# Attention stage of a vision tower: where the short slots of the score pass stand among the steps of the key pass

## The chip, the cores and the metric

The program runs on one core of one Trainium2 chip. The metric is device time in microseconds of that core. The kernel before ran three times: 1735.34, 1737.99 and 1738.87 us, median 1737.99 us. One further execution was recorded by the hardware profiler.

## The reference, cut to what matters

The reference is a small vision tower on 4 sequences of 513 tokens with 192 channels. It has a token embedding, a recurrent mixer with a feed-forward part, an attention layer with a routed expert feed-forward part, a spiking attention, and a last attention layer with a feed-forward part. The two softmax attention layers have 12 heads of 16 channels; the change lies in the function that computes them. For one layer:

```python
scores = jnp.einsum('bqhd,bkhd->bhqk', q, k) / jnp.sqrt(jnp.float32(Dh))
attn = jax.nn.softmax(scores, axis=-1)
ao = jnp.einsum('bhqk,bkhd->bqhd', attn, v).reshape(B, S, D)
```

The second layer (`a = softmax(q k^T * scale)`, `o = a v`) has the same form, sizes and code.

## The kernel before, in words

`attention` (L1922) runs twice, once as `att0` and once as `att1`. The 12 heads of a batch entry are taken four at a time, so one attention is 12 groups of (batch entry, four heads). Every group goes through two passes.

The first pass finds the maximum of the scores of each query. TensorE multiplies queries by keys (`scores`, L2024, 128 queries by 512 keys, one PSUM bank each), and VectorE reduces each bank to one maximum per query (L2149). A group has 16 such units, taken two at a time in 8 full *slots*. Two short slots go with them. `last_queries` (L2037, the unit `ends`) scores the 513th query of the four heads in one bank, which takes VectorE one reduction (L2154). `last_keys` (L2047, the unit `last`) scores all queries against the 513th key, after which VectorE merges all maxima into the tile `mexp` with small instructions (L2162, L2167, L2169). A group has 10 slots (`SLOTS`), numbered u = 0 to 9. Then `turn` (L2065) transposes the maxima of the group on TensorE, and `copy_max` (L1979) copies them as an extra row into the queries: VectorE copies for one half of the partitions, ScalarE for the other. So the second pass gets scores from which the maximum is already subtracted. The banks of units `s`, `ends`, `last` and `max` are the three banks 0 to 2, used in turn in the order of the list `ring`; `free` (L2008) makes TensorE wait until the bank's former content has been read.

The second pass multiplies keys by queries (`keys`, L2085, half of the queries at a time), takes the exponential on ScalarE (L2198, L2195), and multiplies by the values on TensorE (`values`, L2110), adding up in bank 3. It has 10 *steps* per group, 0 to 9: steps 0 to 3 and 5 to 8 have two units each (two calls of `keys`, two exponentials of 514 columns), steps 4 and 9 are short and have one unit (one call for the 513th key, one exponential of 257 columns, L2195). The 18 units of a group are numbered i = 0 to 17; unit 8 and unit 17 are the short ones. `keys` of a unit waits until the exponential of the unit two before it is done, since there are two pairs of banks for it. `values` of a step comes two steps later (`BEHIND`). ScalarE also copies the sums of each half out of bank 3 (`copy_sums`, L2177) after units 3 and 12, and the first `values` of a half waits for that copy (L2118).

TensorE's order is written out by a loop over steps (L2131 to L2140): step t issues `keys`, then the two score units of slot LEAD + t, then `keys` of the second unit, then `values` of step t - 2, then `others` (L2075): `last_queries`, `last_keys` or `turn`, if slot LEAD + t is one of u = SLOTS - 2, SLOTS - 1 or 1. The first LEAD slots are issued ahead of the loop. LEAD is 13 before, so step k of a group has slot u = k + 3 (modulo 10) beside it: `last_queries` (u = 8) stands in step 5, `last_keys` (u = 9) in step 6, `turn` (u = 1) in step 8, and the short steps 4 and 9 carry the full slots u = 7 and u = 2. On ScalarE, `copy_max` for the next group stands after the exponential of unit 15, which is the first unit of step 8. VectorE takes everything in the order of `ring` (L2144).

While `att0` runs, GpSimd splits expert weights into halves beside it (L2487, L2489, L2491, one after the other); `att1` runs without that.

Of the kernel before, what the change touches and what calls it, by code (L numbers as in the profile page):

```python
# [44 lines left out]
SLOTS = (2 * NT + EXPERTS * 127) // 128  # L45
# [1876 lines left out]
def attention(c, name, q2, kT, v, aT, att, wts, experts=False):  # L1922
# [2 lines left out]

    nc = c.nc
    NK = AT
    HALF = T // 2 + 1  # L1930
# [5 lines left out]
    G = len(groups)  # L1936
    with ExitStack() as ctx:
# [9 lines left out]
        NS = len(S_UNITS)  # L1947
        SLOTS = NS // 2 + 2
# [3 lines left out]
        STEP_OF = [i for i, step in enumerate(STEPS) for _ in step]  # L1952
        NB, NT_ = len(UNITS), len(STEPS)
        assert NT_ == SLOTS
        LEAD = SLOTS + 3
        BEHIND = 2
        mc = (mc_v, mc_s)
        acc = c.bank[3]

        ring = []  # L1960
        for n in range(G * SLOTS + 2):
            g, u = divmod(n, SLOTS)
            if g < G and u < SLOTS - 2:
                ring += [("s", g * NS + 2 * u), ("s", g * NS + 2 * u + 1)]
            ring += [("ends", g)] if u == SLOTS - 2 else []
            ring += [("last", g)] if u == SLOTS - 1 else []
            ring += [("max", g - 1, 0), ("max", g - 1, 1)] if u == 1 and g else []
        place = {unit: at for at, unit in enumerate(ring)}

        def bank_of(unit):  # L1970

            return c.bank[place[unit] % 3]
# [6 lines left out]
        def copy_max(eng, copy, g, gi, e):  # L1979

            b, j = groups[g]
            eng.wait_ge(mt, 2 * g + gi + 1)
            bank = bank_of(("max", g, gi))
            r = 64 * e + 32
            copy(q2[r:r + 1, 2 * j + gi, b * T:b * T + KEYS], bank.bitcast(F16)[r:r + 1, 0:KEYS]).then_inc(mc[e], 1)
            copy(q2[r:r + 1, 2 * j + gi, b * T + KEYS:(b + 1) * T], bank[r:r + 1, KEYS - 1:KEYS]).then_inc(mc[e], 1)

        halves = ExpertHalves(c, ctx) if experts else None
        with nc.Block() as block:
            @block.sync  # L1990
            def _(sp):
                if experts:
                    halves.load(sp)
# [13 lines left out]
            def _(pe):  # L2007
                def free(unit):  # L2008

                    at = place[unit]  # L2010
                    if at < 3:
                        return
                    before = ring[at - 3]
                    if before[0] == "s":
                        pe.wait_ge(maxed, before[1] + 1)
                    elif before[0] == "ends":
                        pe.wait_ge(ends_max, before[1] + 1)
                    elif before[0] == "last":
                        pe.wait_ge(placed, 3 * before[1] + 3)
                    else:  # L2020
                        for e in range(2):
                            pe.wait_ge(mc[e], 2 * (2 * before[1] + before[2] + 1))

                def scores(s):  # L2024
                    g, u = divmod(s, SLOTS)
                    if g >= G or u >= SLOTS - 2:
                        return
                    b, j = groups[g]
                    for n in (g * NS + 2 * u, g * NS + 2 * u + 1):
                        gi, k, e = S_UNITS[n % NS]  # L2030
                        q0 = b * T + 128 * k
                        r = slice(64 * e, 64 * e + 64)
                        free(("s", n))
                        pe.matmul(bank_of(("s", n))[:, 0:KEYS], q2[r, 2 * j + gi, q0:q0 + 128],  # L2034
                                  kT[r, 2 * j + gi, b * T:b * T + KEYS], start=True, stop=True).then_inc(scored, 1)

                def last_queries(g):  # L2037
                    b, j = groups[g]
                    free(("ends", g))
                    for gi in range(2):  # L2040
                        for e in range(2):
                            r, to = slice(64 * e, 64 * e + 64), 32 * (2 * gi + e)
                            ins = pe.matmul(bank_of(("ends", g))[to:to + 32, 0:KEYS], q2[r, 2 * j + gi, ends_of(g)],
                                            kT[r, 2 * j + gi, b * T:b * T + KEYS], start=True, stop=True)
                    ins.then_inc(ends, 1)

                def last_keys(g):  # L2047
                    b, j = groups[g]
                    if g == 0:
                        pe.wait_ge(init, 2)  # L2050
                    free(("last", g))
                    bank = bank_of(("last", g))
                    for gi in range(2):
                        for k in range(NK):
                            q0, at = b * T + 128 * k, 2 * (gi * NK + k)
                            pe.matmul(bank[:, at:at + 2], q2[:, 2 * j + gi, q0:q0 + 128], last[:, 2 * j + gi, b, :],
                                      start=True, stop=True)
                    for gi in range(2):
                        for e in range(2):
                            r, to = slice(64 * e, 64 * e + 64), 32 * (2 * gi + e)  # L2060
                            ins = pe.matmul(bank[to:to + 32, 4 * NK:4 * NK + 1], q2[r, 2 * j + gi, ends_of(g)],
                                            last[r, 2 * j + gi, b, e:e + 1], start=True, stop=True)
                    ins.then_inc(lasts, 1)

                def turn(g):  # L2065
                    pe.wait_ge(placed, 3 * g + 3)
                    for gi in range(2):
                        free(("max", g, gi))
                        bank = bank_of(("max", g, gi))
                        for k in range(NK):  # L2070
                            pe.transpose(bank.bitcast(F16)[:, 128 * k:128 * k + 128], mexp[:, g % 2, gi, k, :], idh[:, :])
                        pe.matmul(bank[:, KEYS - 1:KEYS], mexp[:, g % 2, gi, NK, :], one[:, 0:1], start=True, stop=True
                                  ).then_inc(mt, 1)

                def others(s):  # L2075

                    g, u = divmod(s, SLOTS)
                    if u == SLOTS - 2 and g < G:
                        last_queries(g)
                    if u == SLOTS - 1 and g < G:  # L2080
                        last_keys(g)
                    if u == 1 and 1 <= g <= G:
                        turn(g - 1)
# [43 lines left out]

                for s in range(LEAD):
                    scores(s)
                    others(s)  # L2130
                for t in range(G * NT_ + BEHIND):  # L2131
                    g, step = divmod(t, NT_)
                    if g < G:
                        keys(g, FIRST[step])
                        scores(LEAD + t)
                        if len(STEPS[step]) == 2:
                            keys(g, FIRST[step] + 1)
                    if t >= BEHIND:
                        values(t - BEHIND)
                    others(LEAD + t)  # L2140

# [33 lines left out]
            @block.scalar  # L2175
            def _(act):
                def copy_sums(n):  # L2177
                    b, j = groups[n // 2]
                    act.wait_ge(summed, (NK + 1) * (n + 1))
                    if n % 2:  # L2180
                        act.wait_ge(copied, n)
                    at = b * T + START[n % 2]
                    act.copy(aT[:, j, at:at + HALF], acc[:, 0:HALF]).then_inc(copied, 1)  # L2183

                for gi in range(2):
                    copy_max(act, act.copy, 0, gi, 1)
                for n in range(G * NB):
                    g, i = divmod(n, NB)
                    half, k, gi = UNITS[i]
                    act.wait_ge(keyed, n + 1)  # L2190
                    if n >= RING:
                        g0, i0 = divmod(n - RING, NB)
                        act.wait_ge(summed, g0 * NT_ + STEP_OF[i0] + 1)
                    if k == NK:
                        act.activation(p[:, n % RING, 0, :], c.pair[2 + n % 2][:, 0:HALF], ACT.Exp, scale=scale  # L2195
                                       ).then_inc(expd, 1)
                    else:
                        act.activation(p[:, n % RING, :, :],  # L2198
                                       c.pair[2 + n % 2][:, :].rearrange("p (e q) -> p e q", e=2)[:, :, 0:HALF],
                                       ACT.Exp, scale=scale).then_inc(expd, 1)  # L2200
                    if i == NB - 3 and g + 1 < G:
                        for gi in range(2):
                            copy_max(act, act.copy, g + 1, gi, 1)
                    if i == 3 and g:
                        copy_sums(2 * g - 1)
                    if i == 12:
                        copy_sums(2 * g)
                copy_sums(2 * G - 1)
# [1133 lines left out]
```

## Time and profile before

| | |
|---|---|
| time of the runs | 1735.34, 1737.99, 1738.87 us |
| profiled execution: own time | 1737.85 us |
| profiled execution: span | 1736.1 us |
| TensorE matmul busy | 1454.7 us (84%) |
| VectorE busy | 1240.4 us (71%) |
| ScalarE busy | 1015.9 us (59%) |
| GpSimd busy | 407.1 us (23%) |
| VectorE reductions of scores, L2149 | 234.9 us in 384 |
| ScalarE exponentials, L2198 | 211.9 us in 384 |
| TensorE values, L2124 | 123.5 us in 1536 |
| TensorE keys, L2106 | 112.3 us in 768 |
| TensorE scores, L2034 | 107.8 us in 384 |

The span is the time from the first to the last instruction of the profiled execution; its own time is as the other runs are timed. Attention `att0` takes the stretch from 761.5 us to about 940 us of the span, and `att1` the one from about 1404 us to about 1577 us. Busy sums of the two attentions are not told apart in the rows of the table that name a line: each is over both.

### The profile page before, as it was taken

The numbers are of one execution on the slowest core, as the hardware profiler recorded it, in microseconds if no ns is written. First come the engines' busy times: TensorE is split into PE (matmuls) and PEld (weight loads), VectorE is DVE, ScalarE is ACT, GpSimd is POOL, SyncE is SP. The second block draws the span as 40 slices with busy tenths as digits, with TensorE's granted clock in tenths as the row PEclk, the third lists the DMA queues.
The fourth block names the chain that finished last, engine by engine and source line by source line (L and its number), as shares of the span: only waits on it lengthen the run. The fifth ranks groups of instructions, "written<-read, shape, count | busy, mean of one in ns | idle before, by whom it ended". The sixth has DMA issues, their size and how long they took to land. (4 is left out here: it accounts for less than half of the span.)

```text
span 1736.1 us, 36685 instructions
## 1 busy us (share of the span) xinstructions
PE 1454.7 (84%) x14444; PEld 1083.2 (62%) x14444; DVE 1240.4 (71%) x2561; ACT 1015.9 (59%) x1867; POOL 407.1 (23%) x414
## 2 busy tenths in 40 slices
PE   5889898698489789899999719995697999999795
PEld 5889898598455757643335618884586643336474
DVE  5988898389789557468885657874656378885466
ACT  6988898343668264547886306663102448884565
POOL 0000000101556220349920117763000310000200
PEclk9999999689699989879999759998697879999897
DMA  5110100100000100015500732121200000000101
GB/s 147 29 42 29 38 2 11 45 1 1 1 9 2 32 4 15 1 59 183 171 30 2 213 118 60 58 63 34 70 1 14 1 1 2 2 2 2 35 1 37
DMA packets 52750, 67.98 MB, mean 39 GB/s; under 512 B 11536, under 2 KB 41490, under 8 KB 52579
## 3 DMA queue, kind: packets, MB, share of 16 engines
q1 hardware_dynamic: 46022, 50.30, 9.6%
q0 software_dynamic: 3840, 9.18, 1.8%
q10 hardware_dynamic: 2716, 6.14, 1.4%
q8 instruction: 116, 1.90, 0.5%
q14 instruction: 56, 0.45, 0.1%
HBM read 46.97 MB, written 18.65 MB: 38 GB/s over the span
## 5 line engine op out<-in xcount | busy, mean ns | idle before, releaser
L340 PE MATMUL banks<-tok_wT,feature_halves 128*128 128x192 f16 x2592 | 229.3, 249 | 23.7 <-DVE feature_halves L366 12.5
L2149 DVE TENSOR_REDUCE att_max<-banks 128x1 f32<-128x512 f32 x384 | 234.9, 682 | 6.9 <-PE banks L2034 5.9
L340 PEld LDWEIGHTS banks<-tok_wT,feature_halves 128*128 128x128 f16 x2592 | 216.8, 99 | 33.0 <-DVE feature_halves L366 18.3
L2198 ACT ACTIVATE att_p<-banks 128x514 f32<-128x514 f32 x384 | 211.9, 600 | 30.9 <-PE banks L2106 22.8
L366 DVE TENSOR_TENSOR feature_halves<-features,feature_halves 128x2048 f16<-128x2048 f32 x54 | 123.4, 2286 | 6.9 <-ACT feature_halves L463 6.9
L2124 PE MATMUL banks<-att_p,att_v 128*32 128x257 f32 x1536 | 123.5, 394 | 0.5 <-ACT att_aT L2183 0.3
L2106 PE MATMUL banks<-att_q,att_kT 64*128 64x257 f16 x768 | 112.3, 282 | 6.0 <-ACT att_p L2198 3.1
L2034 PE MATMUL banks<-att_kT,att_q 64*128 64x512 f16 x384 | 107.8, 416 | 9.8 <-PEq L1793 4.0
L135 PE MATMUL banks<-ones 128*128 128x256 f16 x654 | 88.7, 294 | 28.4 <-PEq L252 13.7
L463 ACT CAST feature_halves<-features 128x2048 f16<-128x2048 f32 x54 | 102.3, 1894 | 11.3 <-PE banks L340 10.5
L135 PEld LDWEIGHTS banks<-ones 128*128 128x128 f16 x654 | 65.7, 105 | 46.4 <-issue 25.3
L2106 PEld LDWEIGHTS banks<-att_q,att_kT 64*128 64x128 f16 x768 | 36.7, 94 | 85.8 <-ACT att_p L2198 51.8
L2923 ACT COPY slot_xT<-banks 128x512 f16<-128x512 f16 x40 | 23.4, 586 | 94.4 <-PE banks L2873 91.7
L2886 PE MATMUL banks<-slot_xT,expert_w 128*128 128x128 f16 x1200 | 75.3, 222 | 3.0 <-ACT slot_xT L2923 2.9
L741 POOL MEMSET xT<- 1x4104 f32 x1 | 3.5, 3519 | 313.2 <-POOLq L252 313.2
L2886 PEld LDWEIGHTS banks<-slot_xT,expert_w 128*128 128x128 f16 x1200 | 70.6, 99 | 6.1 <-ACT slot_xT L2923 5.9
L355 DVE SCALAR_TENSOR_TENSOR angle_rest<-raw_T,freq,turns 128x1024 f32<-128x1024 f32 x54 | 69.1, 1279 | 6.2 <-ACT turns L240 5.7
L2902 PE MATMUL banks<-expert_w,slot_hidden_halves 128*128 128x192 f16 x720 | 65.9, 246 | 8.9 <-DVE slot_hidden_halves L2971 8.4
L2902 PEld LDWEIGHTS banks<-expert_w,slot_hidden_halves 128*128 128x128 f16 x720 | 58.2, 97 | 12.9 <-issue 9.8
L2840 POOL DMA_INDIRECT slot_x<-token_rows,slot_comes x40 | 46.8, 1169 | 74.5 <-POOLq L2541 62.7
L2034 PEld LDWEIGHTS banks<-att_kT,att_q 64*128 64x128 f16 x384 | 31.1, 95 | 48.8 <-DVE att_max L2149 20.5
L456 ACT ACTIVATE features<-angle_abs,half_pi 128x1024 f32<-128x1024 f32 x54 | 61.5, 1138 | 0.0
(493 smaller groups left out, 3487.2 us busy)
## 6 DMA issues: line engine op xcount, KB each, us to landing
expert_w_in<-in_L_ffn_w_dram SPq DMA_DIRECT2D x16, 576.0 KB, 4.6
expert_w_halves<-expert_w_halves SPq DMA_DIRECT2D x32, 288.0 KB, 2.4
tok_w<-in_L_tok_W_dram ACTq DMA_DIRECT2D x4, 1152.0 KB, 7.2
expert_w2s<-expert_w_halves SPq DMA_DIRECT2D x1, 4608.0 KB
expert_y<-expert_out SPq DMA_DIRECT2D x6, 513.0 KB
expert_w1s<-expert_w_halves SPq DMA_DIRECT2D x2, 1536.0 KB
raw<-in_x_dram SPq DMA_DIRECT2D x2, 1152.0 KB, 5.5
expert_w1s<-expert_w_halves SPq DMA_DIRECT2D x3, 768.0 KB
```

The costliest lines, as they stand in the source:

```text
L135: pe.matmul(c.bank[bank][:, 0:256], ones[:, 0:128], ones, start=True, stop=True)
L340: ins = pe.matmul(c.bank[t // 2][:, (t % 2) * D:(t % 2 + 1) * D], fh[:, s, q, z, t * 128:(t + 1) * 128], wT[:, y, k, 6 * q + wf, :], start ...
L355: own.did(dve.scalar_tensor_tensor(fr[:, n % 2, :], rT[:, k, hf * HALF:(hf + 1) * HALF], freq_col(k, f), fm[:, n % 2, :], ALU.mult, ALU.su ...
L366: dve.tensor_tensor(fh[:, s, :, 1, :], feat[:, s, :, :], fh[:, s, :, 0, :], ALU.subtract).then_inc(flow, 1)
L463: act.copy(fh[:, s, :, 0, :], feat[:, s, :, :]).then_inc(fhigh, 1)
L2034: pe.matmul(bank_of(("s", n))[:, 0:KEYS], q2[r, 2 * j + gi, q0:q0 + 128], kT[r, 2 * j + gi, b * T:b * T + KEYS], start=True, stop=True).th ...
L2106: ins = pe.matmul(c.pair[2 + n % 2][:, 512 * e:512 * e + HALF], kT[r, 2 * j + gi, k0:k0 + 128], q2[r, 2 * j + gi, queries], start=True, st ...
L2124: ins = pe.matmul(acc[32 * hh:32 * hh + 32, 0:HALF], v[:, b, k, 4 * j + hh, :], p[:, (n + hh // 2) % RING, hh % 2, :], start=(k == 0), sto ...
L2149: dve.reduce_max(mx[:, n // NS % 2, 2 * gi + e, k:k + 1], bank_of(unit)[:, 0:KEYS], X).then_inc(maxed, 1)
L2198: act.activation(p[:, n % RING, :, :], c.pair[2 + n % 2][:, :].rearrange("p (e q) -> p e q", e=2)[:, :, 0:HALF], ACT.Exp, scale=scale).the ...
L2886: ins = pe.matmul(ps, ws[:, s, at:at + 128], xt[:, s, b, :], start=(k == 0), stop=(k == len(TERMS) - 1))
L2902: ins = pe.matmul(ps, hh[:, s, a, f, :], w2[:, f, b, :], start=(f == k == 0), stop=(f == NF - 1 and k == 2))
```

## The change

The unit `ends` moves from u = 8 to u = 4 (`ENDS = NK`), and the score units of u = 5 to 8 follow it (`first_score`). LEAD grows from 13 to 15. With that, step k has slot u = k + 5 (modulo 10) beside it: `last_keys` (u = 9) stands in step 4, `turn` (u = 1) in step 6, `last_queries` (u = 4) in step 9, and the eight full slots stand in the eight full steps. ScalarE's `copy_max` moves from after unit 15 to after unit 11, the first unit of step 6. No instruction is added or taken away.

```diff
-        LEAD = SLOTS + 3
+        ENDS = NK
+        LEAD = SLOTS + NK + 1
         BEHIND = 2
...
+        def first_score(g, u):
+
+            return g * NS + 2 * (u - (u > ENDS))
+
         ring = []
         for n in range(G * SLOTS + 2):
             g, u = divmod(n, SLOTS)
-            if g < G and u < SLOTS - 2:
-                ring += [("s", g * NS + 2 * u), ("s", g * NS + 2 * u + 1)]
-            ring += [("ends", g)] if u == SLOTS - 2 else []
+            if g < G and u not in (ENDS, SLOTS - 1):
+                n0 = first_score(g, u)
+                ring += [("s", n0), ("s", n0 + 1)]
+            ring += [("ends", g)] if u == ENDS and g < G else []
             ring += [("last", g)] if u == SLOTS - 1 else []
             ring += [("max", g - 1, 0), ("max", g - 1, 1)] if u == 1 and g else []
...
                 def scores(s):
                     g, u = divmod(s, SLOTS)
-                    if g >= G or u >= SLOTS - 2:
+                    if g >= G or u in (ENDS, SLOTS - 1):
                         return
                     b, j = groups[g]
-                    for n in (g * NS + 2 * u, g * NS + 2 * u + 1):
+                    for n in (first_score(g, u), first_score(g, u) + 1):
...
                 def others(s):
 
                     g, u = divmod(s, SLOTS)
-                    if u == SLOTS - 2 and g < G:
+                    if u == ENDS and g < G:
                         last_queries(g)
...
-                    if i == NB - 3 and g + 1 < G:
+                    if i == NB - 7 and g + 1 < G:
                         for gi in range(2):
                             copy_max(act, act.copy, g + 1, gi, 1)
```

## Rows read from the trace of the kernel before

**Rows 1.** The page, part 1: busy us, share of the span, instructions.
```profile
PE 1454.7 (84%) x14444; PEld 1083.2 (62%) x14444; DVE 1240.4 (71%) x2561; ACT 1015.9 (59%) x1867; POOL 407.1 (23%) x414
```
**Rows 2.** Timeline of VectorE in att1: start us, us, instruction, [idle before <-releaser].
```profile
1506.48 0.69 DVE L2154 TENSOR_REDUCE att_max_last<-banks 128x1 f32<-128x512 f32 x1 [0.53 <-PE banks L2043]
1508.08 0.16 DVE L2162 TENSOR_TENSOR att_max_last<-att_max_last,banks 128x1 f32<-128x1 f32 x1 [0.91 <-PE banks L2061]
...
1508.30 0.23 DVE L2169 TENSOR_SCALAR att_max_placed<-consts,att_max_last 128x4 f16<-128x4 f32 x1
...
1511.87 7.30 DVE L2149 TENSOR_REDUCE att_max<-banks 128x1 f32<-128x512 f32 x12
1519.69 0.69 DVE L2154 TENSOR_REDUCE att_max_last<-banks 128x1 f32<-128x512 f32 x1 [0.53 <-PE banks L2043]
```
**Rows 3.** Timeline of TensorE in the same group of att1.
```profile
1507.40 0.35 PE L2056 MATMUL banks<-att_last_keys,att_q 128*128 128x2 f16 x8
...
1507.80 0.28 PE L2106 MATMUL banks<-att_q,att_kT 64*128 64x257 f16 x2
...
1508.91 0.28 PE L2106 MATMUL banks<-att_q,att_kT 64*128 64x257 f16 x2
...
1510.17 0.40 PE L2071 MATMUL banks<-att_ident,att_max_placed 128*128 128x128 f16 x4
...
1510.75 0.29 PE L2099 MATMUL banks<-att_q,att_kT 64*32 64x257 f16 x4
...
1511.81 0.64 PE L2124 MATMUL banks<-att_p,att_v 128*32 128x257 f32 x8
1512.56 0.29 PE L2106 MATMUL banks<-att_q,att_kT 64*128 64x257 f16 x2
...
1517.23 0.29 PE L2099 MATMUL banks<-att_q,att_kT 64*32 64x257 f16 x4
```
**Rows 4.** Timeline of ScalarE in the same group.
```profile
1510.62 0.58 ACT L1985 COPY att_q<-banks 1x512 f16<-1x512 f16 x1 [0.78 <-PE banks L2072]
...
1511.82 0.60 ACT L2198 ACTIVATE att_p<-banks 128x514 f32<-128x514 f32 x1
1512.31 0.38 ACT L2195 ACTIVATE att_p<-banks 128x257 f32<-128x257 f32 x1
...
1514.99 0.38 ACT L2183 COPY att_aT<-banks 128x257 f32<-128x257 f32 x1
```
**Rows 5.** Timeline of TensorE, last group of att0: a short step without scores, then one more.
```profile
932.44 0.29 PE L2099 MATMUL banks<-att_q,att_kT 64*32 64x257 f16 x4
932.66 0.64 PE L2124 MATMUL banks<-att_p,att_v 128*32 128x257 f32 x8
933.24 0.40 PE L2106 MATMUL banks<-att_q,att_kT 64*128 64x257 f16 x4
```
**Rows 6.** Timeline of VectorE in att0, beside GpSimd's work: two groups.
```profile
787.34 2.62 DVE L2169 TENSOR_SCALAR att_max_placed<-consts,att_max_last 128x4 f16<-128x4 f32 x1
...
829.78 0.78 DVE L2169 TENSOR_SCALAR att_max_placed<-consts,att_max_last 128x4 f16<-128x4 f32 x1
```
**Rows 7.** Timeline of GpSimd in att0, at the same places.
```profile
786.80 3.12 POOL L2487 TENSOR_SCALAR expert_w_in<-expert_w_in 128x1152 f32<-128x1152 f32 x1
789.99 1.14 POOL L2489 CAST expert_w_halves<-expert_w_in 128x1152 f16<-128x1152 f32 x1
791.22 2.37 POOL L2491 TENSOR_TENSOR expert_w_halves<-expert_w_in,expert_w_halves 128x1152 f16<-128x1152 f32 x1
...
827.41 3.12 POOL L2487 TENSOR_SCALAR expert_w_in<-expert_w_in 128x1152 f32<-128x1152 f32 x1
```
**Rows 8.** Timeline of TensorE, att1: the first keys after the leading slots.
```profile
1418.01 0.72 PE L2106 MATMUL banks<-att_q,att_kT 64*128 64x257 f16 x2
```
**Rows 9.** Timeline of ScalarE, att1: the first exponentials.
```profile
1418.10 1.28 ACT L2198 ACT_TABLE_LOAD   x1
1419.40 2.82 ACT L2198 ACTIVATE att_p<-banks 128x514 f32<-128x514 f32 x5
```
## The prediction

> **What bounds the kernel now.** I read the page first: TensorE is busy 84% of the span, VectorE 71%, ScalarE 59% [rows 1]. The change touches only the two attentions, so what counts is what ends last inside one group of them. I went to the timelines of the three engines over one group of att1, which GpSimd leaves alone. The reader is to see a pattern that repeats: the reduction of `ends` starts at 1506.48 and the next at 1519.69, so a group takes 13.21 us [rows 2]. There are 24 such groups, 22 with a turn of maxima inside the steps (11 in each attention).
>
> VectorE is idle 0.53 + 0.91 = 1.44 us of a group, before the reduction of `ends` and before the merge after `last` [rows 2]. Those are the steps in which it gets no full slot. It reduces a bank each 7.30/12 = 0.61 us, so a full slot is 1.22 us to it. TensorE takes 1.11 us for a full step with scores (1507.80 to 1508.91) [rows 3] and hardly pauses, except in one place. That place is the turn: it starts at 1510.17, ScalarE, idle for 0.78, starts its copies at 1510.62 and is back at exponentials only at 1511.82 [rows 3, 4]. TensorE's keys of the next group start at 1512.56, 0.14 after the end of that exponential (1511.82 + 0.60 = 1512.42): they wait for it. Meanwhile TensorE had `values` of step 7 to do, issued at 1511.81 [rows 3]. So a group is no engine's pure work; it is a round of three engines with one stop at the copies of maxima and smaller ones at the short slots.
>
> **The change part by part.** No instruction comes or goes, so the sum is one of waits. I lay the group out anew with the distances of the rows, starting from `last_keys`, set at 1507.40 in both.
>
> From `last_keys` to the turn nothing changes. Before, steps 7 and 8 follow it; after, steps 5 and 6, which have the same contents (two units, one full slot). `last_keys` takes 0.40 (to 1507.80), the next step 1.11, and the turn again starts at 1510.17 and ends at 1510.75 [rows 3]. ScalarE copies after the first unit of that step in both versions, so it is again free at 1511.82 [rows 4]. VectorE's merge and its reductions keep their order, too.
>
> Then comes what is new. Before, the step after the turn is the short step 9: keys of unit 17, a full slot, `values`. The keys that need the exponential delayed by the copies stand behind those `values`. After, it is the full step 7: keys of unit 13, a slot, *keys of unit 14*, `values` of step 5. Keys of unit 14 need the exponential of unit 12, which is the one behind the copies, so they start at 1512.56, where step 0 starts today. `values` of step 5, 0.58 of work [rows 5], are queued behind them. They also need `copy_sums` of the first half, which stands right behind unit 12's exponential: start 1512.31 (the next instruction starts 0.49 after the exponential), 0.38 long, 0.14 for the signal, so 1512.83 [rows 4]; after keys at 1512.56 + 0.22 [rows 5] it would be 1512.78. Step 7 ends at 1512.83 + 0.58 = 1513.41, where before step 9 was over at 1512.56. Slip: 0.85.
>
> From there to the next `last_keys`, before: 1507.40 + 13.21 - 1512.56 = 8.05. After: step 8 at 1.11; step 9 without scores at 0.22 + 0.58 [rows 5] and `last_queries` at no more than the 0.40 of `last_keys`, 1.20; steps 0 to 3 at 1517.23 - 1512.56 = 4.67 [rows 3]; step 4 up to `last_keys` at 0.22 + 0.58 = 0.80. Sum 7.78, so 0.27 is gained by the waits that went from the former steps 5 and 6. That is all that the alignment gives: a short step costs TensorE its `values` in any case, and VectorE's 1.44 idle time was not what TensorE waited for.
>
> One more term. Today the slot of step 0 is begun by VectorE at 1511.87 + 1.22 = 1513.09, 0.53 after the step [rows 2, 3]. After, the reduction of `ends` stands before it and can't begin before `last_queries` is done, at the start of step 0; it takes 0.61, and VectorE's 1.22 per slot is more than TensorE's 4.67/4 = 1.17 per step. TensorE is three banks ahead at most. I bound this by 0 (lag absorbed) and 0.25 (0.2 later at step 0, then 0.05 a step), and take 0.10, nearer to nothing, since the waits of ScalarE lie in the same steps. Per group: 0.85 - 0.27 + 0.10 = 0.68; ends 0.50 - 0.15 (should step 8 and 0 win back another 0.4 of the slip, for ScalarE has two exponentials in hand) = 0.15 below, and 0.85 above. Times 22: 15.0 us (3.3 to 18.7).
>
> LEAD 15 puts one full slot and one `ends` more ahead of the first keys: three reductions, 1.83. Behind them stand the first keys, now at 1418.01 [rows 8]. But the first exponential starts at 1419.40, behind the table load from 1418.10 [rows 9], which no keys are needed for; some 0.9 of the 1.83 lies beside it. I take 1.0 for each attention, 2.0 in all (0 to 4; the two slots less at the end had nobody waiting).
>
> In att0 there is GpSimd. L2169 alone takes 0.23 [rows 2]. Beside GpSimd it took 2.62 and ended at 789.96, and 0.78 and ended at 830.56 [rows 6]; GpSimd's L2487 ended at 789.92 and 830.53 [rows 7]. So it waits out the GpSimd instruction under way. The two places are 40.60 apart, three groups at 13.53, and GpSimd's own are 40.61 apart, six rounds at 6.77: a group of 13.21 plus a wait has locked to two rounds, at a wait of 0.55, of which 13.53 - 13.21 = 0.32 shows. A group of 13.9 is over 13.54 and can't lock so. Then L2169 falls anywhere in three instructions with hardly a gap [rows 7]: mean wait (3.12² + 1.14² + 2.37²)/(2 x 6.77) = 1.23, of which 1.0 shows. Seven groups run beside GpSimd. Before: 2.39 - 0.23 = 2.2 for the first and 6 x 0.32, 4.1; after: 7.0. Plus 3 us (-3, if it falls in gaps, to +10, if it meets the start of the instructions each time).
> The Trainium skill, page "SBUF — State Buffer", section "Who interferes with whom", says that VectorE and GpSimd share a pair of ports as an exclusive lock, that `tensor_scalar` in a two-port mode takes it, and that `tensor_reduce` never does. By that rule, the trace agrees: L2169 is a TENSOR_SCALAR, the reductions kept 0.61. By the rule the phase between the two engines decides, and the sum would be that of the rows; by the 0.23 of the undisturbed row it would be 3 us lower.
>
> Sum: 15.0 + 2.0 + 3 = 20 us on the profiled execution's own 1737.85, which is the median of 1737.99 but for 0.14. Forecast 1758.
>
> **The rivals.**
> *The slip is won back.* 0.5 of the waits in the 8.05 us after it go (8.05 against 7.5 of pure steps): 0.35 a group, 22 x 0.35 = 7.7, leads 2: 1747. For it: ScalarE has units 13 and 14 in hand. Against: TensorE's own steps take 1.11 whatever ScalarE has.
> *GpSimd's lock.* L2169 meets the start of each instruction: about 1.9 more shown wait in five of seven groups, +9.5 for my +3: 1765. For it: 13.85 is close over 13.54, so it would drift by 0.3 a group into the next instruction. Against: it can only happen while GpSimd works.
> *Faster, the other side.* VectorE sets the group. If the small waits of TensorE for banks are really VectorE's 1.44, filling the short steps takes off up to that, and the stop at the copies is covered as now: 0.85 slip less 1.44 is -0.6 a group, x 22 = -13: 1725. It decides if TensorE's full steps today are stretched by VectorE by over 0.1 each. For it: VectorE's 1.22 per slot is over TensorE's 1.11. Against: steps 0 to 3 together are only 0.23 over 4 x 1.11.
> *No effect.* The slip of 0.58 for `values` is just work shifted, and all of it comes back: 1738. Against: it leaves TensorE idle from about 1511.8 to 1512.83, where now it works.
>
> **How the numbers follow.** Forecast 0.48, won back 0.20, lock 0.13, faster 0.12, no effect 0.07. Slower by over 0.2% (3.5 us, about what a measurement tells from none) is 0.81, within it 0.07, faster 0.12. The range leaves out the faster case and no effect, 0.19: from 1741 (3.3 for the groups, nothing else) to 1770 (18.7 + 4 + 9.5). The likeliest case alone: 1750 to 1764.
>
> **What would show it.** In att1, a group of 13.8 to 13.9 instead of 13.21. In step 7 (the step after the turn), a pause of TensorE of about 0.7 ahead of the second keys, waiting for L2198, and `values` behind it at 2.1 from the turn's end. ScalarE's copies, the exponential and `copy_sums` in one row. VectorE idle some 0.5 before each short slot still, plus some 0.8 in step 8. L2169 of changing length in att0. The prediction is wrong if the group is below 13.3: then step 7's `values` didn't wait, or the steps today are stretched by VectorE. It is wrong in size if `values` start at once after the keys but steps 0 to 3 shrink below 4.5.

## The result

The changed kernel takes 1764.55 us (median of 4 runs, 1761.2 to 1766.32), the kernel before 1736.66 us (4 runs, 1735.01 to 1738.87). The ratio is 1.0159, 95% interval 1.0136 to 1.0181: slower, by 28 us between the medians. The forecast was 1758 with a range of 1741 to 1770. The profiled execution of the changed kernel has a span of 1763.4 us, 27.3 us over that of before. Its page, part 1 (answers to [rows 1]):

```profile
span 1763.4 us, 36685 instructions
PE 1470.3 (83%) x14444; PEld 1080.6 (61%) x14444; DVE 1250.6 (71%) x2561; ACT 1020.2 (58%) x1867; POOL 410.4 (23%) x414
```

The shares of the span show nothing of where the time went: the engines have the same instructions and wait more. So I measured each attention in the profiled executions, from the end of VectorE's last copy into `kT` to the end of ScalarE's last copy of sums:

| | before | after | difference |
|---|---|---|---|
| ahead of att0 | 759.9 | 761.2 | +1.3 |
| att0 | 180.1 | 200.7 | +20.6 |
| between the attentions | 461.9 | 457.5 | -4.4 |
| att1 | 175.6 | 184.8 | +9.2 |

The stretch between the attentions isn't touched by the change; over the profiled executions of this study it lay anywhere from 453.7 to 462.8 us. Differences of whole runs of a few us carry that noise, so what follows goes by groups and attentions.

**A group in att1.** VectorE's timeline of the changed kernel (answers to [rows 2]). The reduction of `ends` (now L2161) starts 13.89 us apart, where it was 13.21; VectorE now idles three times, 0.54, 0.75 and 0.78.

```profile
1509.27 0.69 DVE L2161 TENSOR_REDUCE att_max_last<-banks 128x1 f32<-128x512 f32 x1 [0.54 <-PE banks L2050]
...
1515.49 0.16 DVE L2169 TENSOR_TENSOR att_max_last<-att_max_last,banks 128x1 f32<-128x1 f32 x1 [0.75 <-PE banks L2068]
...
1521.34 1.29 DVE L2156 TENSOR_REDUCE att_max<-banks 128x1 f32<-128x512 f32 x2 [0.78 <-PE banks L2041]
1523.16 0.69 DVE L2161 TENSOR_REDUCE att_max_last<-banks 128x1 f32<-128x512 f32 x1 [0.54 <-PE banks L2050]
```

TensorE's timeline from one `last_keys` to the next (answers to [rows 3]). The turn ends at 1518.16, where step 7 begins; its score units are held up (0.91), its second keys start at 1519.88 behind a pause of 0.60, and `values` at 1520.23.

```profile
1514.80 0.35 PE L2063 MATMUL banks<-att_last_keys,att_q 128*128 128x2 f16 x8
...
1518.16 0.29 PE L2113 MATMUL banks<-att_q,att_kT 64*128 64x257 f16 x2
1518.38 0.91 PE L2041 MATMUL banks<-att_kT,att_q 64*128 64x512 f16 x2
1519.88 0.29 PE L2113 MATMUL banks<-att_q,att_kT 64*128 64x257 f16 x2 [0.60 <-ACT att_p L2205]
1520.23 0.64 PE L2131 MATMUL banks<-att_p,att_v 128*32 128x257 f32 x8
1520.80 0.29 PE L2113 MATMUL banks<-att_q,att_kT 64*128 64x257 f16 x2
...
1523.04 0.28 PE L2113 MATMUL banks<-att_q,att_kT 64*128 64x257 f16 x2
...
1527.90 0.29 PE L2106 MATMUL banks<-att_q,att_kT 64*32 64x257 f16 x4
...
1528.69 0.35 PE L2063 MATMUL banks<-att_last_keys,att_q 128*128 128x2 f16 x8
```

ScalarE's timeline of the same place (answers to [rows 4]): four copies of maxima, then the exponential of unit 12, then the copy of the sums.

```profile
1518.02 0.58 ACT L1992 COPY att_q<-banks 1x512 f16<-1x512 f16 x1 [0.78 <-PE banks L2079]
...
1519.22 0.60 ACT L2205 ACTIVATE att_p<-banks 128x514 f32<-128x514 f32 x1
1519.72 0.37 ACT L2190 COPY att_aT<-banks 128x257 f32<-128x257 f32 x1
```

**A group in att0.** The starts of the reduction of `ends` beside GpSimd's work are 15.13, 18.25, 15.51, 18.48, 15.37 and 16.40 us apart, and 13.9 after it; before, they were 15.30 apart once and then 13.5 to 13.7. The 15.13 is the first group after the leading slots, which is about as long in att1 (15.58); the other five are the ones lengthened. VectorE's TENSOR_SCALAR (L2176, answers to [rows 6]) waits for GpSimd's instruction (answers to [rows 7]), and TensorE for it:

```profile
802.04 2.89 DVE L2176 TENSOR_SCALAR att_max_placed<-consts,att_max_last 128x4 f16<-128x4 f32 x1
```
```profile
801.78 3.12 POOL L2494 TENSOR_SCALAR expert_w_in<-expert_w_in 128x1152 f32<-128x1152 f32 x1
```
```profile
804.99 0.73 PE L2041 MATMUL banks<-att_kT,att_q 64*128 64x512 f16 x2 [2.06 <-DVE att_max_placed L2176]
```

And there is more in these groups than the wait. The next rows give the busy time by stretches of the changed kernel: start and end, length, busy us and instructions of TensorE, its weight loads, VectorE, ScalarE and GpSimd, then the granted clock of TensorE, DMA share, GB/s. The first row is the stretch around the pause, the second the one behind it. TensorE is busy 2.74 of 4.80 us at a granted clock of 1.00, and then the clock is 0.51, near its lower level of 1.2 GHz, for 6.7 us. The same happened at 840.5 to 847, behind the wait of L2176 at 835.80, and not at 874 to 880, behind the one at 869.65.

```profile
801.50:806.30 4.80, 2.74 (x32) 0.84 (x32) 4.48 (x7) 1.69 (x3) 4.65 (x4) 1.00 0.73 246
806.90:813.60 6.70, 6.32 (x48) 1.58 (x45) 3.64 (x9) 4.50 (x11) 6.55 (x4) 0.51 0.51 176
...
840.50:847.00 6.50, 6.12 (x48) 1.63 (x45) 3.89 (x9) 4.62 (x11) 6.35 (x4) 0.53 0.59 181
...
874.00:880.00 6.00, 5.20 (x64) 2.03 (x60) 4.62 (x11) 4.69 (x12) 5.85 (x4) 1.00 0.27 101
```

### The profile page after: what moved, and what is told of

Read it like the earlier page. It is cut to its first block and busy times, and to the rows that moved or that the text cites. A ratio compares the mean times of both kernels' runs of the same rounds, so it can differ in the third digit from the quotient of the medians.

```text
span 1763.4 us, 36685 instructions
## 1 busy us (share of the span) xinstructions
PE 1470.3 (83%) x14444; PEld 1080.6 (61%) x14444; DVE 1250.6 (71%) x2561; ACT 1020.2 (58%) x1867; POOL 410.4 (23%) x414
## 5 line engine op out<-in xcount | busy, mean ns | idle before, releaser
L2156 DVE TENSOR_REDUCE att_max<-banks 128x1 f32<-128x512 f32 x384 | 237.7, 682 | 24.1 <-PE banks L2041 23.4
L340 PE MATMUL banks<-tok_wT,feature_halves 128*128 128x192 f16 x2592 | 228.2, 248 | 23.3 <-DVE feature_halves L366 12.2
L2113 PE MATMUL banks<-att_q,att_kT 64*128 64x257 f16 x768 | 120.2, 287 | 15.9 <-ACT att_p L2205 15.6
L2131 PE MATMUL banks<-att_p,att_v 128*32 128x257 f32 x1536 | 127.8, 406 | 2.0 <-ACT att_aT L2190 0.7
L2041 PE MATMUL banks<-att_kT,att_q 64*128 64x512 f16 x384 | 114.9, 424 | 16.5 <-DVE att_max_placed L2176 8.6
L2909 PE MATMUL banks<-expert_w,slot_hidden_halves 128*128 128x192 f16 x720 | 66.3, 246 | 10.5 <-DVE slot_hidden_halves L2978 8.9
L2847 POOL DMA_INDIRECT slot_x<-token_rows,slot_comes x40 | 53.2, 1329 | 73.2 <-POOLq L2548 61.5
L1827 PE MATMUL banks<-att_qkv_w,xT 96*128 96x384 f32 (+3 forms) x136 | 57.4, 548 | 5.6 <-POOL att_qkv_parts L1802 3.1
```

Source lines behind the costliest of these rows:

```text
L340: ins = pe.matmul(c.bank[t // 2][:, (t % 2) * D:(t % 2 + 1) * D], fh[:, s, q, z, t * 128:(t + 1) * 128], wT[:, y, k, 6 * q + wf, :], start ...
L2113: ins = pe.matmul(c.pair[2 + n % 2][:, 512 * e:512 * e + HALF], kT[r, 2 * j + gi, k0:k0 + 128], q2[r, 2 * j + gi, queries], start=True, st ...
L2131: ins = pe.matmul(acc[32 * hh:32 * hh + 32, 0:HALF], v[:, b, k, 4 * j + hh, :], p[:, (n + hh // 2) % RING, hh % 2, :], start=(k == 0), sto ...
L2156: dve.reduce_max(mx[:, n // NS % 2, 2 * gi + e, k:k + 1], bank_of(unit)[:, 0:KEYS], X).then_inc(maxed, 1)
L2909: ins = pe.matmul(ps, hh[:, s, a, f, :], w2[:, f, b, :], start=(f == k == 0), stop=(f == NF - 1 and k == 2))
```

## The experiments

Each is timed against runs of the kernel before made beside it (medians 1735.71 for e1 to e4, 1738.85 for e5 to e8, 1740.08 for e9; e9 has two runs of its own, the others four to ten). The ratio is the one on record, which differs from the quotient of the two medians by up to 0.002. The group is the distance of the starts of the `ends` reduction in the steady part of att1; att0 and att1 are from one profiled execution each.

| kernel | time, us | ratio to before, 95% | group | att0 | att1 |
|---|---|---|---|---|---|
| before | 1736.66 | | 13.21 | 180.1 | 175.6 |
| after | 1764.55 | 1.0159 (1.0136 to 1.0181) | 13.89 | 200.7 | 184.8 |
| e1, sums copied first | 1761.0 | 1.0162 (1.0127 to 1.0196) | 13.84 | 194.3 | 186.9 |
| e2, maxima copied after unit 12 | 1737.6 | 1.0018 (0.9997 to 1.0038) | 13.21 | 179.6 | 177.2 |
| e3, after with fused merge | 1749.37 | 1.0084 (1.0060 to 1.0108) | 13.82 | 183.9 | 183.9 |
| e4, before with fused merge | 1725.25 | 0.9944 (0.9925 to 0.9962) | 13.15 | 174.6 | 174.4 |
| e5, turn back in step 8 | 1741.08 | 1.0010 (0.9998 to 1.0023) | 13.1 | 183.9 | 177.3 |
| e6, e5 and maxima after unit 16 | 1726.62 | 0.9939 (0.9920 to 0.9958) | 12.52 | 179.4 | 170.4 |
| e7, before, maxima after unit 16 | 1736.53 | 0.9982 (0.9956 to 1.0008) | 13.18 | 179.7 | 174.4 |
| e8, e6 with fused merge | 1722.19 | 0.9907 (0.9890 to 0.9924) | 12.45 | 170.0 | 169.5 |
| e9, after with filler matmuls | 1786.52 | 1.0271 (1.0211 to 1.0330) | 15.27 | 208.3 | 202.4 |

**e1: is it the copy of the sums that `values` wait for?**

```diff
+                    if i == 11:
+                        copy_sums(2 * g)
                     if i == NB - 7 and g + 1 < G:
...
-                    if i == 12:
-                        copy_sums(2 * g)
```

> The changed kernel, with the copy of the first half's sums moved on ScalarE from behind the exponential of unit 12 to ahead of the copies of maxima (after unit 11). Theory A (the keys of unit 14 wait for the exponential of unit 12, which is queued behind the copies of maxima, and the values stand behind these keys): the sums are now free early, but the keys of unit 14 start no earlier, and the values follow them 0.35 us later as today; the group of att1 stays at 13.8 to 13.9 us and the time at 1762 to 1765 us. Rival B (what stops TensorE in step 7 is the wait of the values for the copied sums): the pause behind the turn goes, the group falls by 0.5 to 0.8 us to 13.1 to 13.4, the time by 11 to 18 us to about 1750.

The group is 13.84, so B falls; the time of 1761.0 is 1 us under what A expected. TensorE's timeline of e1 behind the turn: the sums are copied before the maxima now, yet the second keys still wait for the exponential, and `values` stand behind them. They follow the keys by 0.21 where it was 0.35, so the copied sums did hold `values` in the changed kernel, but the second keys come 0.09 later here, and 0.05 a group is all that remains.

```profile
1540.21 0.29 PE L2113 MATMUL banks<-att_q,att_kT 64*128 64x257 f16 x2
1540.42 0.91 PE L2041 MATMUL banks<-att_kT,att_q 64*128 64x512 f16 x2
1542.02 0.28 PE L2113 MATMUL banks<-att_q,att_kT 64*128 64x257 f16 x2 [0.69 <-ACT att_p L2205]
1542.23 0.64 PE L2131 MATMUL banks<-att_p,att_v 128*32 128x257 f32 x8
```

**e2: take the copies of maxima out of the way of unit 12.**

```diff
-                    if i == NB - 7 and g + 1 < G:
-                        for gi in range(2):
-                            copy_max(act, act.copy, g + 1, gi, 1)
...
                     if i == 12:
                         copy_sums(2 * g)
+                    if i == NB - 6 and g + 1 < G:
+                        for gi in range(2):
+                            copy_max(act, act.copy, g + 1, gi, 1)
```

> The changed kernel, with ScalarE's copies of maxima moved from behind unit 11 to behind unit 12 and behind the copy of the sums, so that the exponential of unit 12 runs in the 0.78 us in which ScalarE waits for the turn. Theory A: keys of unit 14 start right behind the score units of step 7, values at once behind them; the 0.7 to 0.8 us pause goes, the group of att1 falls from 13.89 to 13.0 to 13.2 us, 22 x 0.75 = 17 us less, 1747 us or, if in att0 VectorE's L2176 meets GpSimd more kindly, down to 1735. Rival B gives the same as in the run before. Rival C (full slots beside full steps stretch TensorE's steps, and the turn has no part in it): the group stays above 13.6 us, 1760 us.

The group falls by 0.68 to 13.21, at the upper end of what was expected, and the kernel is as fast as the one before (1.0018). Three moved lines of ScalarE's order take back the whole loss in the group; in att0 the groups are again at 13.5, locked to GpSimd. So the aligned slots, even without the pause behind the turn, gain nothing over the kernel before. TensorE's timeline of e2: there is no pause ahead of the second keys (1494.89), but the score units of step 7 still take 0.91, and step 7 is 1.80 long (1494.15 to 1495.95), not 1.11. The weight load of the second score unit shows what it waits for: VectorE's copies of maxima out of its bank (last line, of the timeline of the weight loads).

```profile
1494.15 0.29 PE L2113 MATMUL banks<-att_q,att_kT 64*128 64x257 f16 x2
1494.36 0.91 PE L2041 MATMUL banks<-att_kT,att_q 64*128 64x512 f16 x2
1494.89 0.49 PE L2113 MATMUL banks<-att_q,att_kT 64*128 64x257 f16 x2
1495.31 0.64 PE L2131 MATMUL banks<-att_p,att_v 128*32 128x257 f32 x8
1495.95 0.29 PE L2113 MATMUL banks<-att_q,att_kT 64*128 64x257 f16 x2
```
```profile
1494.87 0.09 PEld L2041 LDWEIGHTS banks<-att_kT,att_q 64*128 64x128 f16 x1 [0.43 <-DVE att_q L1993]
```

**e3 and e4: take the lock away, in both kernels.** The merge of the last query's maximum (L2169 of the changed kernel) and its placing by TENSOR_SCALAR (L2176, the L2169 of before) become one instruction. It reads the bank in PSUM and, in SBUF, the tile `ident` and one value per partition:

```diff
-                        dve.tensor_tensor(mlast[:, g % 2, 1:2], mlast[:, g % 2, 0:1], bank_of(unit)[:, 4 * NK:4 * NK + 1],
-                                          ALU.max).then_inc(last_max, 1)
...
-                        dve.wait_ge(last_max, g + 1)
-                        dve.tensor_scalar(mexp[:, g % 2, :, NK, 32:128:64],
-                                          c.const("ident")[:, 31:128:32].rearrange("p (i e) -> p i e", e=2),
-                                          mlast[:, g % 2, 1:2], None, ALU.mult).then_inc(placed, 1)
+                        dve.scalar_tensor_tensor(mexp[:, g % 2, :, NK, 32:128:64],
+                                                 bank_of(unit)[:, 4 * NK:4 * NK + 1].unsqueeze(2).broadcast_to((128, 2, 2)),
+                                                 mlast[:, g % 2, 0:1],
+                                                 c.const("ident")[:, 31:128:32].rearrange("p (i e) -> p i e", e=2),
+                                                 ALU.max, ALU.mult).then_inc(placed, 1)
```

> The changed kernel, with L2169 and L2176 (the merge of the 513th query's maximum and its placing by TENSOR_SCALAR) made one scalar_tensor_tensor that reads the bank in PSUM and one operand in SBUF. Theory D (in att0 TENSOR_SCALAR waits out the GpSimd instruction under way, TensorE idles up to 2 us behind it, and its granted clock is 0.51 for about 7 us in every second group): no such wait, no fall of the clock; the groups of att0 fall from 15.1 to 18.5 us to 13.8 to 13.9, which is 14 to 15 us less, 1749 us; att1 stays at 13.8 to 13.9. Rival E (GpSimd slows VectorE or the clock falls whatever this instruction is): groups of att0 stay above 15 us, the time within 4 us of the changed kernel's 1764.

> The kernel before, with the same fused merge. Theory D: the groups of att0 fall from 13.53 us (15.30 in the first) to the 13.2 us of att1, 4 us in all: 1733 us, and against the changed kernel with the fused merge the change then costs 22 x 0.68 + 2 = 17 us rather than 27. Rival E: no difference from the kernel before.

D holds and E falls. With the fused merge every steady group of att0 takes as long as one of att1: 13.82 in e3, 13.15 in e4. The edit changes the operation and where its operands lie at once, so it doesn't tell which of the two ends the waiting; in the changed kernel the TENSOR_TENSOR beside it (L2174, one operand in SBUF and one in PSUM) kept its 0.18 us all along. VectorE's timeline of e3 in att0 shows the new instruction at 0.23 in the middle of GpSimd's work:

```profile
812.80 0.26 DVE L2172 TENSOR_TENSOR att_max_placed<-att_max,banks 128x8 f16<-128x8 f32 x2 [0.75 <-PE banks L2068]
812.95 0.23 DVE L2173 SCALAR_TENSOR_TENSOR att_max_placed<-banks,att_max_last,consts 128x4 f16<-128x4 f32 x1
```

The stretch from 780 to 880 us, of the changed kernel and of e3, has a mean granted clock of 0.90 and 0.98.

```profile
780.00:880.00 100.00, 87.45 (x966) 30.25 (x962) 82.10 (x152) 68.00 (x144) 97.70 (x46) 0.90 0.52 167
```
```profile
780.00:880.00 100.00, 94.41 (x1156) 35.04 (x1159) 83.72 (x172) 80.83 (x172) 96.90 (x45) 0.98 0.51 167
```

The pair also gives the change's price without the waits for GpSimd: att0 183.9 - 174.6 = 9.3, att1 183.9 - 174.4 = 9.5, 19 us in all, where 17 was expected. The medians of the two kernels are 24.1 apart; the 5 us between that and the attentions of the profiled executions are not explained. The fused merge saves 5.5 us in att0 of the kernel before and 16.8 in att0 of the changed one, so the lock, with what follows from it, makes up 11.3 of the 20.6 us lost there. e4 is 10.5 us faster than the kernel before (1735.71 in the runs beside it), of which the attentions give 6.6, where 4 was expected in all; in its profiled execution the stretch between them was 8.2 us shorter, and whether more than the noise told of above is in that isn't shown.

**e5 and e6: keep the alignment, move the turn.** e5 puts the turn two slots later (u = 3, so step 8) and ScalarE's copies back behind unit 15; e6 puts them behind unit 16.

```diff
-        for n in range(G * SLOTS + 2):
+        for n in range(G * SLOTS + 4):
...
-            ring += [("max", g - 1, 0), ("max", g - 1, 1)] if u == 1 and g else []
+            ring += [("max", g - 1, 0), ("max", g - 1, 1)] if u == 3 and g else []
...
-                    if u == 1 and 1 <= g <= G:
+                    if u == 3 and 1 <= g <= G:
...
-                    if i == NB - 7 and g + 1 < G:
+                    if i == NB - 2 and g + 1 < G:
```

(NB - 3 in e5.)

> The changed kernel, with the turn of maxima back in step 8 (two slots later in the order of the banks, u = 3) and ScalarE's copies of maxima back behind unit 15; the short slots stay on the short steps. Theory A (the alignment itself gains about 0.27 us a group, and the loss came from the turn standing ahead of a full step): what follows the turn is again a short step with one call of keys and then values; a group of att1 takes 12.9 to 13.1 us, 22 x 0.2 = 4 us less than the kernel before, with 1 to 2 us lost in each attention ahead of the first keys: 1734 us. Rival C (full slots beside full steps stretch the steps): 13.5 us or more, 1745 us.

> As the run before, and ScalarE's copies stand behind unit 16, so that its exponential runs while ScalarE waits for the turn. Theory A: the keys of the next group no longer wait for the exponential of unit 16; the group falls by up to 0.6 us to 12.4 to 12.6 us and is then near VectorE's own work of a group (12.2 us, 13.9 less its idle time), 1722 us. Rival C: no more than 0.1 us under the run before.

e5's group is 13.1, and C falls: the 13.5 or more that it foretold did not come. But e5 gains 0.1 a group, not 0.2, and att1 is 1.7 us longer than before, since its first exponential comes 17.57 us after the first reduction, where it was 15.25. In att0 it also meets GpSimd once for 2.58 us, and its clock is at half for 3.4 us behind that. The kernel is the same as before (1.0010), 7 us above what was expected. TensorE in e5 has done everything else when it waits for the exponential behind the copies:

```profile
1529.18 0.40 PE L2050 MATMUL banks<-att_kT,att_q 64*32 64x512 f16 x4
1530.19 0.29 PE L2113 MATMUL banks<-att_q,att_kT 64*128 64x257 f16 x2 [0.62 <-ACT att_p L2205]
```

e6 takes that wait away: 12.52 a group, as expected, and faster than before (0.9939), though in att0 its groups stay at 13.53, two GpSimd rounds; the time, 1726.62, is 5 above what was expected. What bounds a group then is TensorE: it is busy all 12.52 us of one, VectorE 11.58 (not the 12.2 of the expectation).

```profile
1490.42:1502.94 12.52, 12.52 (x164) 4.91 (x163) 11.58 (x25) 11.12 (x25) 0.00 (x0) 1.00 0.01 2
```

**e7: the kernel before, with the copies behind unit 16** (`NB - 3` becomes `NB - 2` in its line).

> The kernel before, with ScalarE's copies of maxima behind unit 16 instead of unit 15. Theory A: the keys of the next group no longer wait for that exponential, but TensorE had values of step 7 to do until 0.17 us before it, so only 0.15 us a group is gained: 13.05 us in att1, 1732 to 1735 us. In att0 the lock to two GpSimd rounds holds at 13.53 us, so that half of it doesn't show.

13.18: it gains 0.03 of the 0.15 expected, no difference in the time. There the score units of step 9, still 0.90 long, stand ahead of `values` and wait for VectorE's copies of maxima:

```profile
1510.93 0.09 PEld L2034 LDWEIGHTS banks<-att_kT,att_q 64*128 64x128 f16 x1 [0.42 <-DVE att_q L1986]
```

Step 0 does start 0.19 us sooner behind the turn than before, but steps 0 to 3 then take 4.82 instead of 4.67. The turn stands in step 8 in the kernel before and in e5, e6 and e7 alike. So moving the short slots alone (e5) gives 0.1, moving the copies alone (e7) 0.03, and both together (e6) 0.69: behind the turn stand the score units, which wait for their bank, and the keys, which wait for the exponential, and taking away one wait leaves the other.

**e8: e6 with the fused merge.**

> The run of the turn at u = 3 with copies behind unit 16, and the fused merge (scalar_tensor_tensor in place of L2169 and L2176). Theories A and D together: groups of 12.3 to 12.5 us in both attentions, no fall of the clock in att0; 22 x 0.8 = 17 us and 4 us of the lock less than the kernel before, plus 2 us of the longer lead: 1716 us. If VectorE's slots behind the copies become the bound instead, 12.8 us and 1724 us.

12.45 us a group in both attentions, 1722.19 us, ratio 0.9907: faster than both kernels. The groups came out as expected; the time is 6 above. Half of that is the kernel before, which ran 3 us slower beside it than beside e1 to e4; and the first exponential comes 17.50 us after the first reduction, 2.3 an attention later than before, where 1 was allowed for. TensorE's timeline of e8 from the turn to step 0, which starts at 1499.01 straight behind `last_queries`: the turn's copies cost it nothing.

```profile
1497.31 0.40 PE L2078 MATMUL banks<-att_ident,att_max_placed 128*128 128x128 f16 x4
...
1498.68 0.40 PE L2050 MATMUL banks<-att_kT,att_q 64*32 64x512 f16 x4
1499.01 0.29 PE L2113 MATMUL banks<-att_q,att_kT 64*128 64x257 f16 x2
```

**e9: does TensorE's pause bring its clock down?**

```diff
+        blank = c.sb(ctx, name + "_blank", [128, 128], F16)
...
+        idle = c.ones[:, :].bitcast(F16)
...
+                pool.memset(blank[:, :], 0.0).then_inc(blanked, 1)
...
                         keys(g, FIRST[step])
+                        if step == 6:
+                            for _ in range(12):
+                                pe.matmul(acc[:, 0:HALF - 1], blank[:, :], idle[:, :], start=False, stop=False,
+                                          skip_group_check=True)
                         scores(LEAD + t)
```

> The changed kernel, with 12 matmuls of 256 columns by a matrix of zeros, added to bank 3 (they add nothing to the sums), between the first keys of step 6 and its score units, where TensorE idles 2.06 us when VectorE's L2176 waits for GpSimd. Every group gets some 1.3 us more work for it, so the time is higher (22 x 1.2 = 26 us, 1780 to 1795 us). Theory F (the granted clock falls to 1.2 GHz behind L2176's long waits because TensorE does too little there): the pause shrinks to under 1 us and the clock stays at 1.00 in all steady groups of att0, though L2176 still takes 2.5 to 3.1 us in some of them. Rival G (the fall comes with the wait of the other engines, whatever TensorE does in it): groups with L2176 above 2.5 us still show a granted clock of about 0.5 for some 7 us behind it.

L2185 (the former L2176) took 2.91 and 2.97 us in two steady groups. TensorE's pause there was 0.66 and 0.71, these groups took 16.3 and 16.4 us against 15.27 in the quiet ones, and the clock stayed at 1.00. TensorE's timeline and the stretch behind the first of them:

```profile
819.78 1.49 PE L2149 MATMUL banks<-ones,att_blank 128*128 128x256 f16 x12
821.92 0.73 PE L2045 MATMUL banks<-att_kT,att_q 64*128 64x512 f16 x2 [0.66 <-DVE att_max_placed L2185]
```
```profile
822.00:829.00 7.00, 6.20 (x70) 2.31 (x72) 5.62 (x13) 4.51 (x11) 6.85 (x4) 1.00 0.59 177
```

The time and the group (1.38 more) are as expected. This speaks for F: two long waits with TensorE kept busy and no fall, against two falls in three long waits without. The other traces add cases. e1 had two such pauses, 2.21 and 2.19 us, and a fall behind the first (row below); four shorter ones, 1.54 to 1.85 us in the kernel before, e5, e6 and e7, brought one fall of 3.4 us, in e5. Each fall began 1.7 to 2.0 us after the end of the pause. And the clock also fell where nobody waited for GpSimd: near the end of att1 in e1, from 1583.0 for 6.8 us, and near the end of att0 of the changed kernel, from 946.6 for 3.4 us. There the score units have run out, and TensorE was busy 5.68 of the 7.00 us before the one and 6.31 of the 8.00 us before the other. So a fall doesn't need a wait for GpSimd. With so few cases it isn't proof, the more so as two of the five pauses over 2 us brought no fall.

```profile
791.10:797.90 6.80, 6.33 (x48) 1.52 (x45) 3.70 (x9) 4.46 (x11) 6.65 (x4) 0.50 0.51 174
```

## Why the prediction was right, and where its size was off

**The slip in step 7** (0.85 a group): right, in mechanism and size. From `last_keys` to the end of step 7 it was to be 6.01 (1507.40 to 1513.41 on its clock) and is 6.00 (1514.80 to 1520.80). It said that keys of unit 14 need the exponential behind the copies, and that the copied sums let `values` go 0.05 later than these keys alone would (1512.83 against 1512.78). e1, with the sums out of the way, gains that 0.05, and e2, with the exponential out of the way, the whole 0.68.

**The gain at the short slots** (0.27) and **VectorE's lag at step 0** (0.10): from the end of step 7 to the next `last_keys` the sum was 7.78 + 0.10 = 7.88, and the trace has 7.89. Inside it steps 0 to 3 took 4.86 (1523.04 to 1527.90), 0.19 over the 4.67 of before where 0.10 was allowed for, and step 9 took 1.12 rather than 1.20: two small errors that cancel, by luck. The group of 13.89 is the predicted one. The lower end of the range for a group doesn't come out of its own line (0.50 - 0.15 is not 0.15; 0.85 - 0.27 - 0.4 gives 0.18), which changes nothing here.

**The lead** (1.0 an attention): in att1 the first exponential comes 16.40 us after the first reduction (1421.64 to 1438.04), before 15.25 (1404.15 to 1419.40): 1.15. Together with the groups the prediction had 8.5 an attention; att1 lost 9.2, and the two attentions 9.3 and 9.5 with the fused merge. The rest is in the first group: from its first exponential to the next group's it lost 1.67 (14.19 to 15.86), not 0.68, and the last such distance lost only 0.35. The prediction left out one thing that lies there: TensorE's granted clock is at half from the start of each attention, for 20.5 us before (from 1403.5) and for 23.9 after (from 1421.1), so into the first group. What of the 1.67 that makes, no run tells.

**GpSimd's lock** (3 us): this is the step that was off, by its size. The working said that the new group is longer than two GpSimd rounds and can't lock so, took the arrivals of TENSOR_SCALAR as spread evenly, and gave a mean wait of 1.23. In fact beyond its own 0.23 it waited 2.66, 1.61, 2.75, 1.48 and 2.75 us in a row, 2.25 on average: three times it came 0.2 to 0.3 us into GpSimd's L2494 of 3.12 us, and twice in between 0.6 to 0.7 us into L2498 of 2.38 us. That looks like a lock again, of two groups to five rounds: the three long ones ended at 804.93, 838.78 and 872.63, 33.85 us apart both times, which is 5 x 6.77. In e1 the two long ones ended 33.83 apart (789.20 and 823.03). The waits are those of the rival "GpSimd's lock", with its 1.9 a group, which I gave 0.13. Even that left out the second half: in two of these groups TensorE's granted clock fell to near 0.5 for over 6 us. They took 4.4 and 4.6 us over 13.89, where the third wait of 2.75, without the fall, cost 2.5; so about 2 us each is the clock's, as an estimate. The fall near the end of att0 cost about 1.2 more: from the first exponential of the last group but one to that of the last it took 14.68 us, where it took 13.45 in att1. The lock and what came with it cost 11.3 us by e3 and e4, where the prediction had 3.

**The rivals.** "Faster" supposed that TensorE's steps were stretched by VectorE and that the copies were covered; neither was so, but e6 and e8 show that its aim was reachable: with the turn in step 8 and the copies one unit later a group takes 12.5. "Won back" and "no effect" fall with 13.89. In the attentions of the profiled executions 17 + 3 was forecast, and they lost 29.8: 18.8 by the pair e3 and e4, which leaves 11.0 for GpSimd. The untouched stretches gave back 2.5 of it (27.3 in the span).

## What to carry to other kernels

When a schedule is shifted, look first at where its one long dependency chain (here: turn, copies, the exponential behind them) comes to stand and what is queued in order behind it; 0.68 us a group was lost there (e2 won it back), against 0.1 gained by fitting short pieces to short steps alone (e5). An instruction that waits for its partner should stand on its engine behind whatever else could run in the wait (here one exponential in 0.78 us of idle time), and when two waits stand behind one another, both must go before either shows (0.1 and 0.03 alone, 0.69 together). A loop that runs beside another one with its own period may be locked to it, and not only one to one: look at whether a few of its periods, waits included, fill a whole number of the other's rounds. An even spread of arrivals was wrong here by a factor of almost four in the cost, the falls of the clock included.

## What the runs showed of the hardware

A VectorE TENSOR_SCALAR of 4 columns, both operands in SBUF, took 0.23 us alone and up to 3.10 us beside GpSimd (e1), ending with the GpSimd instruction under way. In the same stretch of the changed kernel, 780 to 880 us, VectorE's other instructions took as long as without GpSimd: reductions from PSUM 0.67 to 0.69 us, started every 0.61, and a TENSOR_TENSOR with one operand in SBUF and one in PSUM 0.18. A scalar_tensor_tensor that reads PSUM, a tile in SBUF and one value per partition in SBUF took 0.23 in all 24 cases of e3. Behind pauses of TensorE of 2.06 to 2.21 us, with the granted clock at 1.00, the clock was at half for 6.8 us in three cases of five, beginning 1.7 to 2.0 us after the pause; a steady group of the changed kernel with such a fall lost 4.4 to 4.6 us, where the same wait without it cost 2.5.
